# The last attention pass of a graph network with its softmax made in chunks beside the gathers, and its scores scattered and scanned

## What is computed

```python
def _gat_conv(x, W, a_src, a_dst, b, src, dst, n):
    xw = x @ W
    e = jax.nn.leaky_relu((xw @ a_src)[src] + (xw @ a_dst)[dst], 0.2)
    m = jax.ops.segment_max(e, dst, num_segments=n)
    ex = jnp.exp(e - m[dst])
    s = jax.ops.segment_sum(ex, dst, num_segments=n)
    alpha = ex / (s[dst] + 1e-16)
    agg = jax.ops.segment_sum(alpha[:, None] * xw[src], dst, num_segments=n)
    return agg + b
```

## Time and profile before

| | us |
|---|---|
| median of 3 runs | 3219.77 (3218.48 to 3219.83) |
| the profiled execution's own time | 3219.89 |
| its span in the profile | 3218.0 |
| first gather of the last pass to the first instruction of the next stage on GpSimd | 2362.46 to 2972.66 |
| the same of layer 0's pass | 440.01 to 1003.91 |

### The profile page before, as it was taken

One profiled execution on the slowest core, in us unless ns is written; L12 is line 12 of the kernel. 1 busy time (PEld: TensorE's weight loads), 2 busy tenths in 40 slices (PEclk: granted clock), 3 DMA queues, 4 the chain that ended last, 5 costly groups with the idle time before them and its releaser, 6 DMA issues. The chain is left out here.

```text
span 3218.0 us, 44601 instructions
## 1 busy us (share of the span) xinstructions
PE 2481.7 (77%) x12282; PEld 1848.6 (57%) x12282; DVE 1432.4 (45%) x3430; ACT 1058.0 (33%) x2707; POOL 1378.1 (43%) x1389
## 2 busy tenths in 40 slices
PE   2399945777776998999995788787566788776896
PEld 2366524544544776888884455454455666554575
DVE  4664415656656220000004311233467665555767
ACT  1012224444443112232222444444410654443220
POOL 1012247777760041000004577777640677776210
PEclk7599977878877899999998799889765999998898
DMA  5035544444430013656563433333276233333101
GB/s 187 6 123 167 177 126 112 114 113 111 115 98 29 1 65 127 193 183 194 182 195 108 123 105 106 106 106 105 72 250 220 83 100 102 103 102 97 61 1 40
DMA packets 241045, 370.76 MB, mean 115 GB/s; under 512 B 65140, under 2 KB 171073, under 8 KB 240836
## 3 DMA queue, kind: packets, MB, share of 16 engines
q0 software_dynamic: 63632, 179.42, 18.9%
q1 hardware_dynamic: 147694, 157.81, 15.5%
q10 hardware_dynamic: 29510, 31.06, 2.8%
...
...
## 5 line engine op out<-in xcount | busy, mean ns | idle before, releaser
L1089 POOL DMA_INDIRECT ag_rows<-rows,e_bsrc x392 | 392.5, 1001 | 245.6 <-SPq L1100 109.6
L1310 POOL DMA_INDIRECT at_rows<-values,e_brow x392 | 395.1, 1008 | 144.2 <-issue 96.3
L2539 POOL DMA_INDIRECT cm_rows<-rows,e_bsrc x392 | 371.9, 949 | 145.6 <-issue 85.7
L1386 PE MATMUL at_part<-at_msg,x 128*128 128x265 f32 x880 | 279.4, 464 | 82.4 <-DVE at_msg L1541 51.1
L2619 PE MATMUL cm_part<-cm_rows,cm_one 128*128 x880 | 263.5, 436 | 100.0 <-SPq L2546 77.8
L1115 PE MATMUL banks<-ag_msg,ag_one 128*128 128x258 f32 x880 | 242.1, 410 | 103.9 <-DVE ag_msg L1148 53.9
L2619 PEld LDWEIGHTS cm_part<-cm_rows,cm_one 128*128 128x128 f32 x880 | 170.0, 210 | 185.2 <-issue 166.0
L1386 PEld LDWEIGHTS at_part<-at_msg,x 128*128 128x128 f32 x880 | 183.5, 225 | 156.2 <-DVE at_msg L1541 75.9
...
L1115 PEld LDWEIGHTS banks<-ag_msg,ag_one 128*128 128x128 f32 x880 | 167.1, 200 | 164.8 <-issue 74.2
L2742 DVE TENSOR_TENSOR h<-h,cm_part 128x256 f32 x220 | 92.4, 420 | 360.8 <-PE cm_part L2619 331.8
L1984 PE MATMUL x_up<-x_xt,x_w 128*128 128x256 f32 x1024 | 228.1, 381 | 7.5 <-DMA x_b<-in_L_ffn_b2p 7.5
...
## 6 DMA issues: line engine op xcount, KB each, us to landing
...
```

The lines of the kernel that those rows point to most:

```text
L1089: pool.indirect_dma_start(rows[:, b % slots, k, :], None, table, bass.IndirectOffsetOnAxis(index[:, k, b:b + 1], 0)).then_inc(gathered[b % ...
L1310: pool.indirect_dma_start(rows[:, b % RING, k, :], None, table, bass.IndirectOffsetOnAxis(e.block_row[:, k, b:b + 1], 0)).then_inc(gathere ...
L1386: last = pe.matmul(part[:, n % deep, 0:wide], one[:, n // U % 2, k, n % U, :], msg[:, n % 4, k, :], start=(k == 0), stop=(k == K2 - 1))
L2539: pool.indirect_dma_start(rows[:, b % SLOTS, k, :], None, table, bass.IndirectOffsetOnAxis(e.block_src[:, k, b:b + 1], 0)).then_inc(gather ...
```

## The change

- The last pass takes the form of `attend`: `attend_last` makes the softmax in the same 14 chunks, 6 pairs ahead of the messages, beside the gathers, with the self loop's score as floor of the maximum. `score2`, `segment_softmax`, `aggregate`, `low_row` and the masks at the end of `find_groups` go. `find_groups` makes `e.keep` (1 where an edge has the destination of the edge before it) and `e.head` (the destination of each block's first edge) instead.
- The source score rides in the gathered row: `rows2` has 257 columns, and ScalarE copies the last one into `src`.
- The destination score is not matched. `route_and_share` computes `start`, the index of each token's first edge (or a row of no use for a token without edges), by two more pairs of small matmuls and ten small VectorE operations before the end of its list. `gcn_to_gat` scatters each token's destination score and the score of its self loop (8 bytes) to row `start` of `spread_rows`, one indirect DMA for each of the 25 tiles, in groups of five, and stores both by token as well. `spread_rows` is zeroed at the start of the program.
- `attend_last` reads `spread_rows` back block by block, puts the score of each block's first edge in place (two gathers by `e.head`), copies scores forward over the edges of a token with four scans (state × keep + value), stores the result as `block_rows`, gathers it by pair (two gathers, placed after the gathers of the first 8 blocks), stores that as `pair_rows`, and ScalarE's queue fetches each chunk's rows and masks from there.
- The ring is 27 blocks, the slots are freed as in `attend`. The ride's weights load at the start of `attend_last`, and VectorE and TensorE wait for them before the first chunk or message. The ride's down result has one PSUM bank for two.
- In `together` with `gcn_to_gat`, `add` is listed first.

The diff, cut to its core:

```diff
-            link(dve.memset(edge[:, :, 0:1], 0.0))
-            link(dve.tensor_tensor(edge[:, :, 1:BLK], key[:, :, 1:BLK], key[:, :, 0:BLK - 1], ALU.not_equal))
-            link(dve.tensor_reduce(runs[:], edge[:], AX.X, ALU.add))
-            link(dve.tensor_copy(rep[:, :, 0, :], key[:, :, 0:1].broadcast_to([BH, 2, H0])))
-            link(dve.tensor_copy(rep[:, :, 1, :], key[:, :, BLK - 1:BLK].broadcast_to([BH, 2, H0])))
-            dve.tensor_scalar(rep[:, :, 2, :], runs[:].unsqueeze(2).broadcast_to([BH, 2, H0]), 0.0, None, ALU.is_equal).then_inc(ends_made, 1)
-
+            dve.memset(e.keep[:, :, 0:1], 0.0)
+            dve.tensor_tensor(e.keep[:, :, 1:BLK], key[:, :, 1:BLK], key[:, :, 0:BLK - 1], ALU.is_equal)
+            dve.tensor_copy(e.head[:], raw[:, 1, :, 0])
...
             dve.tensor_scalar(one_run[:], e.pair[:, :, 2 * BLK], 0.0, None, ALU.is_equal).then_inc(runs_made, 1)
 
-            link(dve.tensor_scalar(edge[:], edge[:], NEG, None, ALU.mult))
...
-            link(dve.tensor_scalar(e.over_this[:], this[:], -1.0, -NEG, ALU.add, ALU.mult))
             dve.wait_ge(runs_kept, 1)
...
-def segment_softmax(nc, tag, c, e, heads, channels, s, source, out, banks, source_made, s_made, banks_free):
...
-def aggregate(nc, tag, c, e, index, table, heads, weights, acc, slots, banks, gate, ride, ride_ready):
...
+def attend_last(nc, c, e, spread_rows, token_rows, block_rows, pair_rows, table, acc, ride, loads):
...
+            for h in range(2):
+                pool.indirect_dma_start(heads[:, h, :], None, token_rows, bass.IndirectOffsetOnAxis(e.head[:, h:h + 1], 0)).then_inc(heads_in, 16)
+            for b in range(NB):
+                if b == FETCHED:
+                    pool.wait_ge(block_stored, 32)
+                    for h in range(2):
+                        pool.indirect_dma_start(pair_sc[:, h, :], None, block_rows,
+                                                bass.IndirectOffsetOnAxis(e.row[0:HALF, h:h + 1], 0)).then_inc(pair_in, 16)
+                if b >= LAST_RING:
+                    pool.wait_ge(freed, b - LAST_RING + 1)
+                for k in range(K2):
+                    pool.indirect_dma_start(rows[:, b % LAST_RING, k, :], None, table,
+                                            bass.IndirectOffsetOnAxis(e.block_src[:, k, b:b + 1], 0)).then_inc(gathered[b % LAST_RING], 16)
...
+            for h in range(2):
+                sp.dma_start(starts[:, h].rearrange("p e z -> p (e z)"),
+                             spread_rows[h * BH * BLK:(h + 1) * BH * BLK].rearrange("(b e) z -> b (e z)", e=BLK)).then_inc(spread_in, 16)
+            for to, of in loads:
+                sp.dma_start(to, of, allow_slow_non_contiguous=True).then_inc(ride_loaded, 16)
+            sp.wait_ge(filled, 4)
+            for h in range(2):
+                sp.dma_start(block_rows[h * BH:(h + 1) * BH], whole[:, h].rearrange("p z e -> p (z e)")).then_inc(block_stored, 16)
+            sp.wait_ge(pair_in, 32)
+            for h in range(2):
+                sp.dma_start(pair_rows[h * HALF:(h + 1) * HALF], pair_sc[:, h, :]).then_inc(pair_stored, 16)
+            for b in range(NB):
+                sp.wait_ge(gathered[b % LAST_RING], 16 * K2 * (b // LAST_RING + 1))
+                sp.sem_inc(ready, 1)
+                if FREE <= b < NB - LAST_RING + FREE:
+                    pairs = sp.value_load(e.upto[0:1, b - FREE:b - FREE + 1], min_val=1, max_val=G)
+                    sp.wait_ge(weighted, pairs)
+                    sp.sem_inc(freed, 1)
...
+            for n in range(-LEAD, G):
+                if n in step_of:
+                    softmax(*step_of[n])
+                if n < 0:
+                    continue
+                if n == 0:
+                    pe.wait_ge(ride_loaded, 16 * len(loads))
+                ride.multiply(pe, n)
+                if n % U == 0:
+                    pe.wait_ge(hot, n // U + 1)
+                pe.wait_ge(weighted, n + 1)
+                if n >= deep:
+                    pe.wait_ge(summed, n - deep + 1)
+                for k in range(K2):
+                    last = pe.matmul(part[:, n % deep, 0:wide], one[:, n // U % 2, k, n % U, :], msg[:, n % 4, k, :], start=(k == 0), stop=(k == K2 - 1))
+                last.then_inc(multiplied, 1)
...
+            def fetch(n):
+                pc, j = n // CH, n % CH
+                if n % U == 0:
+                    blks[:] = several(nc, mybir.EngineType.Activation, e.blk, n, U, NB - 1, waited=True)
+                b = blks[n % U]
+                if j == 0 and pc >= 2:
+                    act.wait_ge(scored, pc - 1)
+                act.wait_ge(ready, b + 1)
+                act.copy(src[:, pc % 2, :, j:j + 1], rows[:, bass.ds(b % LAST_RING, 1), :, D:D + 1].squeeze(1)).then_inc(copied, 1)
+
+            def softmax(pc, lo, m, i):
+                if i == 3:
+                    act.wait_ge(shifted, pc + 1)
+                    act.activation(s[0:m], s[0:m], ACT.Exp, scale=-1.0).then_inc(exped, 1)
+                if i == 4:
+                    if pc >= 2:
+                        act.wait_ge(weighted, CHUNKS[pc - 1][0])
+                    act.wait_ge(back_turned, pc + 1)
+                    act.copy(w[:, pc % 2, :, 0:m, :].rearrange("p k n z -> p z k n"),
+                             turn[:, 0:2 * K2 * m].rearrange("p (z k n) -> p z k n", z=2, k=K2)).then_inc(w_kept, 1)
+                    if pc + 2 < len(CHUNKS):
+                        take_chunk(pc + 2)
+                if i == 6:
+                    act.wait_ge(faded, pc + 1)
+                    if pc:
+                        act.wait_ge(rescaled, pc)
+                    act.activation(fade[:], small[:, 0:1], ACT.Exp).then_inc(fade_kept, 1)
...
+            hots(0)
+            act.wait_ge(pair_stored, 32)
+            take_chunk(0)
+            take_chunk(1)
+            act.wait_ge(ride_loaded, 16 * len(loads))
+            for n in range(FREE - LEAD):
+                fetch(n)
+            for n in range(-LEAD, G):
+                if n >= 0 and n % U == 0 and n + U < G:
+                    hots(n // U + 1)
+                if n + FREE < G:
+                    fetch(n + FREE)
+                if n in step_of:
+                    softmax(*step_of[n])
+                if n >= 0:
+                    ride.shape(act, n)
...
+                if i == 0:
+                    if pc:
+                        dve.wait_ge(w_kept, pc)
+                        dve.wait_ge(ended, pc)
+                    dve.wait_ge(chunk_in[now], landed_by[pc])
+                    dve.wait_ge(scored, pc + 1)
+                    dve.tensor_tensor(fwd[0:m, :], sc[0:m, now, 0:BLK], turn[0:m, 0:BLK], ALU.add).then_inc(summed_up, 1)
+                    dve.wait_ge(summed_up, pc + 1)
+                    dve.scalar_tensor_tensor(out=s[0:m, 0, :], in0=fwd[0:m, :], scalar=SLOPE, in1=fwd[0:m, :],
+                                             op0=ALU.mult, op1=ALU.max).then_inc(leaked, 1)
+                    dve.wait_ge(leaked, pc + 1)
+                    dve.tensor_tensor_scan(fwd[0:m, :], apart_by[:, 0:BLK], s[0:m, 0, :], 0.0, ALU.add, ALU.max).then_inc(scanned, 1)
+                    dve.wait_ge(scanned, 2 * pc + 1)
+                    dve.tensor_tensor_scan(top[0:m, ::-1], apart_by[:, 1:BLK + 1][:, ::-1], fwd[0:m, ::-1], 0.0,
+                                           ALU.add, ALU.max).then_inc(scanned, 1)
...
+            dve.memset(acc, 0.0).then_inc(cleared, 1)
+            dve.wait_ge(spread_in, 32)
+            dve.wait_ge(heads_in, 32)
+            dve.tensor_copy(starts[:, :, 0, :], heads[:]).then_inc(headed, 1)
+            dve.wait_ge(headed, 1)
+            for h in range(2):
+                for z in range(2):
+                    dve.tensor_tensor_scan(whole[:, h, z, :], e.keep[:, h, :], starts[:, h, :, z], 0.0, ALU.mult, ALU.add).then_inc(filled, 1)
+            dve.wait_ge(cleared, 1)
+            dve.wait_ge(pair_stored, 32)
+            dve.wait_ge(ride_loaded, 16 * len(loads))
...
+                        pe.matmul(place_ps[:, NT * NX:NT * NX + NT], tri[:], degree[:], start=True, stop=True)
+                        pe.matmul(place_ps[:, D + NT * NX:D + NT * NX + NT], c.ones[:], degree[:], start=True, stop=True).then_inc(summed, 1)
...
             dve.tensor_copy(slots[:], row[:]).then_inc(placed, 1)
+            link(dve.tensor_copy(deg[:], place_ps[:, D + NT * NX:D + NT * NX + NT]))
+            link(dve.tensor_tensor_scan(before_it[:], c.ones[:, 0:NT], deg[:], 0.0, ALU.mult, ALU.add))
+            link(dve.tensor_tensor(before_it[:], before_it[:], deg[:], ALU.subtract))
+            link(dve.tensor_tensor(before_it[:], before_it[:], place_ps[:, NT * NX:NT * NX + NT], ALU.add))
+            link(dve.tensor_scalar(dump[:], c.token[:], float(NB * BLK), None, ALU.add))
+            link(dve.tensor_scalar(has[:], degree[:], 1.0, None, ALU.is_ge))
+            link(dve.tensor_tensor(before_it[:], before_it[:], dump[:], ALU.subtract))
```

(34 more changed lines are left out.)

674 lines of the change are left out of this document (231 added, 443 removed).

## The result

The changed kernel takes 3244.9 us (median of 4 runs, 3244.7 to 3247.81), the kernel before 3219.8; the ratio is 1.0079 (1.0062 to 1.0097). The forecast was 3194, with 3178 to 3226. The profiled execution is the longest of the four, 3247.81, its span 3246.0, 28.0 more than before. By the starts of GpSimd's first instruction in each stage those 28.0 are: grouping −6.0 (forecast −4.7), layer 0's pass +3.1 (none; the profiled run lies 2.9 over the median), routing to the experts' end +3.2 (+2.6), convolution +0.7, the stage with the scatters +12.9 (+9.4), the last pass +12.7 (−33.3), what follows +1.3. Nearly all of the miss, 46 of 54 us, is in the last pass.

The account below looks back on a forecast made before the run. The last pass was taken as about 143 us of matching and softmax, then gathers at 1.30 us each. Terms −4.7 + 2.6 + 9.4 − 33.3 = −26.0 took the span 3218.0 to 3192.0, forecast 3194, range 3178 to 3226.

Parts of the forecast that it names:

- −33.3: Last pass: 576.9 us against 610.2, from layer 0's 563.9 plus 5.0 for indirect transfers and 8.0 for the ride.
- Grouping, −4.7: Grouping of edges: VectorE's tail of small operations on ends of runs goes, so the next operation starts 4.7 us sooner.
- Routing, +2.6: Routing: ten linked small operations on VectorE cost 2.2 us and two more pairs of small matmuls 0.4.
- Scatters, +9.4: Stage that makes the table: 25 score scatters on GpSimd end it 9.4 us later, bounds +8 and +13.
- Start of the pass: Last pass: the first weighted message comes about 57 us after the first gather, as in layer 0.
- the margin before the gather by pair: Start of the last pass: block rows are ready about 7 us before GpSimd reaches their gather by pair.
- The ride, +8: Last pass: MLP matmuls carried in the gaps cost 4 us in the stream and 4 in the tail.
- Rival 2: Last pass: a chunk's chain is 1.5 to 2 us longer than its gathers, 3206 to 3226 us; chance 0.20.
- Rival 3: Last pass: 54 changes of table set on ScalarE, all 69.3 us on the path, 3255 us; chance 0.13.
- Rival 4: Last pass: gathers run at 1.25 us each, 24 us less, 3170 us (3164 to 3186); chance 0.10.

Follow-up runs that it names:

- e8_front: Changed kernel with the first 16 of the ride's 103 steps done before the first chunk: 3691.9 us, kernel before 3706.7 on the same chip, ratio 0.9967.
- e10_loads: Kernel before with 27 unread one-column Exps added to ScalarE's list of the last pass, adding 53 table loads: 3222.7 us against 3218.1, ratio 1.0014.

## Why the prediction was wrong

- **Grouping, −4.7:** about right, −6.0 by the first gather of layer 0's pass; the other 1.3 weren't traced. VectorE now waits for the copy, as said. **Routing, +2.6:** about right, 3.2 up to the experts' end. The addition behind the small operations came later, and TensorE's wait for it rose from 1.97 to 4.25 us. Both, VectorE's and TensorE's:

```profile
113.33 0.24 DVE L606 MEMSET e_same<- 1x220 f32 x1 [2.29 <-ACT g_runrows L517]
...
1156.84 1.22 PE L1741 MATMUL ff_down<-ff_w,ff_hid 128*128 128x256 f32 x2 [4.25 <-DVE x L1810]
```

- **Scatters, +9.4:** right in mechanism, and at its upper bound of 13 in size, +12.9. The scatters came 1.29 us apart (forecast 1.27), but from the last one's issue to the next stage are 7.8 us, not the 4.2 taken from the store.
- **Start of the pass:** right, 56.4 us; the margin before the gather by pair held.
- **The ride, +8:** here it failed. The step is "TensorE goes to 381 us in a stream of about 517, so the time holds it", with 4 us allowed in the stream and 4 in the tail. The pass took 54.6 us more than layer 0's from the first message to the last pair's, 4.0 a chunk, and on the slower chips leaving the ride out takes 48 us off. Two things in that step were wrong. It compares a sum with a span: the loop of a chunk is ten pairs of messages and then a chain beside which the other six go, and what stands in the ten pairs counts whether or not TensorE is idle elsewhere; the walk back along the loop has TensorE for 224.5 of 510.1 us, 117.7 of 460.8 in layer 0's. (This is read from traces; without the ride the ten pairs take 27.4 us on the slower chips for 31.1, which agrees, and e8_front, with less of the ride, gained nothing, which doesn't.) And the sum was too small: it took the messages and the ride at the times they had at a granted clock of 0.95, and added of the chunk's matmuls only the first transposes. Measured are 429.7 us up to the next stage, 48.7 more. That the window of the stream alone shows 380.79 is chance, since it holds 1,471 matmuls and the tail another 204. How much of the 54.6 us is the lower clock and how much the place in the loop, no run parts.
- **Rival 2**, the longer period of a chunk, came nearest, at 0.20, and its sign (GpSimd waits for the ring) was there with 54.7 us. Its size was too small (1.5 to 2 us; measured 42.6 − 37.1 = 5.5 over the gathers' pace), and it put the time in another place: in the chain, where it is in the pairs before it. Its argument against itself, "TensorE has 517 − 381 = 136 us to spare in the stream", is the failed step again.
- **Rival 3**, the table loads: 54 as counted, of 1.283 us each. On the slower chips they show no cost that can be told from the 10 us by which one kernel varies. On a chip like that of the result no run of the changed kernel without loads exists; loads can cost their whole time there where a stretch is paced by compute (e10_loads), and the chain through the changed kernel's trace has 25.5 us of them. So they are at most about half of the miss, and how much of it is open. "A load that stands before a Gelu delays only the ride" was wrong in any case: TensorE waits for the Gelu in the list in which the messages stand.
- **Rival 4**, gathers at 1.25: the issue gaps are 0.30 as before, and GpSimd waited for the ring, so the pass didn't go by the gathers' pace.

Of the Trainium skill ("ScalarE: Activation LUTs", section "What ACT_TABLE_LOAD costs") the load's 1283 ns is what the trace has 54 times over; the drain of 1380 ns is not seen: an Exp starts 0.01 us behind its load (2726.87 + 1.28, then 2728.16), and the load 0.02 us behind the copy before it (2726.67 + 0.18).

None of the changed kernel's variants fell on a chip like that of the result, so what the ride costs there isn't measured by a run; it rests on the trace and on the slower chips.
